# Slot attention: W2 and the carried part of o in fp32 on halves of the array's rows, the update of s2 in fp32 on the whole array

## What is computed

```python
s = clip(hs @ Ws1.T @ Ws2.T + bs2, -32, 32)      # heads x rows x 64 slots
es, enz = exp(s), exp(-cumlogsumexp(s))
A  = mask(q @ k.T * scale)
ok = enz * (A @ es)                              # rows x slots
qv = softmax(ok)
W2 = mask((qv * enz) @ es.T)                     # rows x rows, contraction over 64 slots
o  = W2 @ v
out = (rmsnorm(o) * g_norm * silu(g)) @ Wo.T
```

## Time and profile before

| | |
|---|---|
| median of three runs | 1559.19 us |
| lowest, highest | 1558.36, 1561.25 us |
| span of the profiled execution | 1558.6 us |
| PE busy | 1510.6 us, 97% |
| PE weight load busy | 1280.0 us, 82% |
| DVE, ACT, POOL busy | 1038.4, 625.5, 648.5 us |
| mean granted clock of TensorE | 0.992 |
| matmul instructions | 8720 |

### The profile page before, as it was taken

How to read it: one execution, slowest core, us unless ns; L and a number is a source line. 1 busy time by engine, 2 the same in 40 slices (tenths; PEclk the granted TensorE clock), 3 DMA queues, 4 the chain that set the end, 5 groups by cost and what they waited for, 6 DMA issues and landing times.

```text
span 1558.6 us, 24100 instructions
## 1 busy us (share of the span) xinstructions
PE 1510.6 (97%) x8720; PEld 1280.0 (82%) x8720; DVE 1038.4 (67%) x1840; ACT 625.5 (40%) x1235; POOL 648.5 (42%) x641
## 2 busy tenths in 40 slices
PE   7899999999899999999899999999999999999988
PEld 3788888888788888888788888888888888888866
DVE  4766657567676766667866666666776675667667
ACT  5433334335333333333433433333533333433346
POOL 2444343444443443444433434334444443444345
PEclk9999999999999999999999999999999999999999
DMA  8420212013221101202311120212222011201123
GB/s 321 173 78 23 71 44 71 22 62 114 71 71 45 63 29 39 75 27 86 133 49 45 37 77 22 71 44 92 83 68 75 29 64 44 71 22 45 62 81 122
DMA packets 51444, 109.88 MB, mean 70 GB/s; under 512 B 5376, under 2 KB 15616, under 8 KB 46976
## 3 DMA queue, kind: packets, MB, share of 16 engines
q1 hardware_dynamic: 49088, 104.94, 20.1%
q10 hardware_dynamic: 2304, 4.20, 0.7%
HBM read 86.84 MB, written 26.21 MB: 73 GB/s over the span
## 4 chain that ended last, share of the span: by engine, by line
PE 70%; issue 9%; DVE 8%; ACT 6%; POOL 5%; DMA 1%; POOLq 0%; SPq 0%; DVEq 0%; ACTq 0%
PE bank_qv L859 21%; PE bank_kg L859 20%; PE bank_t L873 5%; PE bank_s L977 3%; PE bank_a L859 3%; PE bank_a L896 3%; PE bank_o L1046 3%; PE bank_s L979 3%; PE bank_c L1058 2%; PE bank_o L859 2%; PE bank_s L859 2%; DVE pT_lo L628 2%; ACT pT_hi L475 2%; ACT batch_raw L475 2%; DVE pair_pT_lo L628 1%
## 5 line engine op out<-in xcount | busy, mean ns | idle before, releaser
L395 POOL TENSOR_TENSOR hs_lo<-hs_raw,hs_hi 128x512 fp32r<-128x512 f32 x64 | 81.5, 1274 | 362.5 <-ACT hs_hi L475 362.5
L859 PE MATMUL bank_qv<-w_hi,hs_hi 128*128 128x512 f32 x512 | 210.2, 411 | 12.8 <-issue 6.6
L859 PE MATMUL bank_kg<-w_hi,hs_hi 128*128 128x512 f32 x512 | 208.2, 407 | 1.0 <-DVE rope_b L648 1.0
L859 PE MATMUL bank_qv<-w_hi,hs_lo 128*128 128x512 f32 x512 | 204.4, 399 | 0.0
L859 PE MATMUL bank_qv<-w_lo,hs_hi 128*128 128x512 f32 x512 | 204.2, 399 | 0.0
L859 PE MATMUL bank_kg<-w_hi,hs_lo 128*128 128x512 f32 x512 | 202.2, 395 | 0.0
L859 PE MATMUL bank_kg<-w_lo,hs_hi 128*128 128x512 f32 x512 | 202.2, 395 | 0.0
L475 ACT ACTIVATE oT_hi<-bank_t 128x512 fp32r<-128x512 f32 x65 | 38.8, 597 | 331.6 <-PE bank_t L873 331.6
L400 POOL TENSOR_TENSOR q_rot<-rope_a,rope_b 128x512 f32<-128x512 f32 x64 | 82.3, 1286 | 187.7 <-DVE rope_b L648 187.7
L628 DVE TENSOR_TENSOR pT_lo<-bank_t,pT_hi 64x256 fp32r<-64x256 f32 x128 | 54.0, 422 | 123.3 <-ACT pair_pT_hi L475 122.2
L390 POOL TENSOR_TENSOR v_lo<-batch_raw,ws_low 128x512 fp32r<-128x512 f32 x64 | 82.6, 1290 | 115.0 <-ACT ws_low L475 114.8
(11 more groups left out here) (190 smaller groups left out, 3757.3 us busy)
## 6 DMA issues: line engine op xcount, KB each, us to landing
w_raw<-w_groups SPq DMA_DIRECT2D x32, 1024.0 KB, 4.9
x_scratch<-part SPq DMA_DIRECT2D x65, 256.0 KB, 2.0
hs_raw<-hs_cols SPq DMA_DIRECT2D x64, 256.0 KB, 2.7
part<-x_scratch SPq DMA_DIRECT2D x64, 256.0 KB, 3.1
batch_raw<-hs_cols SPq DMA_DIRECT2D x4, 1024.0 KB, 7.7
u_part<-u_scratch SPq DMA_DIRECT2D x64, 64.0 KB, 2.4
w_raw<-x_scratch SPq DMA_DIRECT2D x16, 256.0 KB, 2.7
x_scratch<-hs_rows SPq DMA_DIRECT2D x1, 3840.0 KB, 16.0
```

What stands on the lines that cost most here:

```text
L395: pool.tensor_tensor(hs_lo[slot][:, :], hs_raw[slot][:, :], hs_hi[slot][:, :].bitcast(F32), ALU.subtract).then_inc(hs_lo_made, 1)
L859: mm = pe.matmul(dst, x, y, start=start and n == 0, stop=stop and n == 2, **kw)
```

## The change

- **W2** becomes four F32 calls (eight matmul instructions), one for each head, with contraction over 64 rows. Head h uses rows 0 to 63 (h even) or 64 to 127 (h odd) of the array and of `esT` and `pT`, which are now plain 128 x 256 F32 tiles, without zeros and without splits.
- **The carried part of o** becomes four such calls on the same halves, with `pT` stationary and `s2` moving. It moves from behind `masked` times v to right behind W2, ahead of `w2_mm`, for which DVE's mask waits.
- **s2** becomes two F32 calls (four instructions), es by v, 256 columns wide, on all 128 rows.
- **PSUM.** `bank_s` and `bank_o` become one tensor, `bank_wo`, of two banks: even heads in the first, odd ones in the second, W2 in columns 0 to 255 of each bank, o in 256 to 511. `slots_acc`, the place of `ok` and of the slots, is in the part of the first bank that o uses later. The out-projection writes `bank_a`, where W2 was.
- **Waits.** W2 waits for `pT_made` (one ACT copy) and for the clip of the next step's slots. `masked` times v waits for the mask alone; the wait for `part_made` stands ahead of the scores. The k transposes wait for ACT's `esT` copy, no longer for a subtraction of DVE.
- **Gone:** on ACT two half copies and a whole one (in place of three, one), and the copy of v; on DVE two subtractions for `pT_lo`, one for `pair_pT_lo`, one for `esT_lo`, two for `s2_lo`; on POOL `v_lo`, and four memsets at the start.

```diff
-                pe.wait_ge(pT_lo_made, i)
-                for r in range(HG // 2):
-                    mm = product(bank_a[:, 2 * P * r:2 * P * r + 2 * P], cols((esT_hi, esT_lo), P * r, P),
-                                 cols((pT_hi, pT_lo), 2 * P * r, 2 * P))
+
+                pe.wait_ge(pT_made, i)
+                if left:
+                    pe.wait_ge(s_clipped, n)
+                for h in range(HG):
+                    rows, at = slice(64 * (h % 2), 64 * (h % 2) + 64), slice(P * (h // 2), P * (h // 2) + P)
+                    mm = pe.matmul(w2_of(h), esT[rows, at], pT[rows, at], start=True, stop=True)
+                if c:
+                    pe.wait_ge(s2_made, carried(u, c - 1))
+                    for h in range(HG):
+                        rows, at = slice(64 * (h % 2), 64 * (h % 2) + 64), slice(P * (h // 2), P * (h // 2) + P)
+                        mm = pe.matmul(o_of(h), pT[rows, at], s2[rows, at], start=False, stop=False,
+                                       skip_group_check=True)
                 mm.then_inc(w2_mm, 1)
...
                 pe.wait_ge(w2_masked, i)
-                pe.wait_ge(part_made, i)
                 for h in range(HG):
                     head = slice(P * h, P * h + P)
-                    mm = pe.matmul(bank_o[:, head], masked[:, head], v[now][:, head], start=h == 0, stop=c == 0,
+                    mm = pe.matmul(o_of(h), masked[:, head], v[now][:, head], start=False, stop=True,
                                    skip_group_check=True)
-                if c:
-                    pe.wait_ge(s2_lo_made, carried(u, c - 1))
-                    for r in range(HG // 2):
-                        mm = product(bank_o[:, 2 * DV * r:2 * DV * r + 2 * DV],
-                                     cols((pair_pT_hi, pair_pT_lo), P * r, P), cols((s2_hi, s2_lo), 2 * DV * r, 2 * DV),
-                                     start=False, skip_group_check=True)
                 mm.then_inc(o_mm, 1)
...
-                    pe.wait_ge(v_lo_made, i)
                     for r in range(HG // 2):
-                        mm = product(bank_s2[:, 2 * DV * r:2 * DV * r + 2 * DV],
-                                     cols((es_hi[now], es_lo[now]), P * r, P),
-                                     cols((v_hi[now], v_lo[now]), 2 * DV * r, 2 * DV),
-                                     start=c == 0 and r == 0, skip_group_check=True)
+                        pair = slice(2 * DV * r, 2 * DV * r + 2 * DV)
+                        mm = pe.matmul(bank_s2[:, pair], es[now][:, P * r:P * r + P], v[now][:, pair],
+                                       start=c == 0 and r == 0, stop=True, skip_group_check=True)
                     mm.then_inc(s2_mm, 1)
                 if left:
+                    pe.wait_ge(part_made, i)
                     scores(n)
```

More of the change, by code:

```diff
@@ L99, in gated_slot_attention_block @@
         k_rot = [sb(f"k_rot{s}", F) for s in range(2)]
-        v_lo = [sb(f"v_lo{s}", F, F32R) for s in range(2)]
         es_hi = [sb(f"es_hi{s}", H, F32R) for s in range(2)]
         es_lo = [sb(f"es_lo{s}", H, F32R) for s in range(2)]
-        esT_hi, esT_lo = sb("esT_hi", H, F32R), sb("esT_lo", H, F32R)
+        esT = sb("esT", H)
         enz = sb("enz", H)
@@ L106, in gated_slot_attention_block @@
         eps_sum, var, rms = sb("eps_sum", HG), sb("var", HG), sb("rms", HG)
-        pT_hi, pT_lo = sb("pT_hi", F, F32R), sb("pT_lo", F, F32R)
-        pair_pT_hi, pair_pT_lo = sb("pair_pT_hi", H, F32R), sb("pair_pT_lo", H, F32R)
-        s2_hi, s2_lo = sb("s2_hi", HG * DV, F32R), sb("s2_lo", HG * DV, F32R)
+        pT, s2 = sb("pT", H), sb("s2", H)
         o_gated = sb("o_gated", F)
@@ L380, in _ @@
                 pool.memset(t[:, :], 1.0).then_inc(ones_set, 1)
[L381 removed]
+            for t in (wo_hi, wo_lo):
                 pool.memset(t[:, :].bitcast(F32), 0.0).then_inc(zeroed, 1)
@@ L583, in step @@
                     from_bank(v[(c + 1) % 2][:, :], bank_qv[:, :], v_mm, n, v_made)
[L584 to L589, removed]
+                from_bank(pT[:, :], bank_t[:, 0:H], pT_mm, i, pT_made)
                 if last and c == 2:
@@ L796, in step @@
                     w_split(WG, g * 4 + 8)
-                dve.wait_ge(pT_hi_made, i)
-                minus_pair(pT_lo, pT_hi, P, lambda half: per_head(bank_t[64 * half:64 * half + 64, 0:H], 2))
-                minus_hi(pair_pT_lo[:, :], bank_t[:, 0:H], pair_pT_hi[:, :]).then_inc(pT_lo_made, 1)
                 if not left:
@@ L827, in step @@
                 if left:
-                    mask(a_mm, n, a_masked)
-                if c < CB - 1:
-                    dve.wait_ge(s2_hi_made, carried(u, c))
-                    minus_pair(s2_lo, s2_hi, DV, lambda half: of_pair(bank_s2[:, :], half, DV)
-                               ).then_inc(s2_lo_made, 1)
+                    mask_a(n)
                 if c == 0:
@@ L930, in _ @@
             pe.wait_ge(u_made, BATCH)
-            pe.matmul(bank_s[:, 0:H], u_part[0][:, :], ws2_part[:, 0:H], start=True, stop=True).then_inc(s_mm, 1)
+            pe.matmul(slots_acc, u_part[0][:, :], ws2_part[:, 0:H], start=True, stop=True).then_inc(s_mm, 1)
             w_ready(4)
@@ L998, in step @@
                     pe.wait_ge(u_in[nxt], (u * 2 + ((c + 1) // 2 + 1)) * 16)
-                    pe.matmul(bank_s[:, 0:H], u_part[nxt][:, :], ws2_cols(g, last and c == CB - 1), start=True,
+                    pe.matmul(slots_acc, u_part[nxt][:, :], ws2_cols(g, last and c == CB - 1), start=True,
                               stop=True).then_inc(s_mm, 1)
```

106 lines of the change are left out of this document (53 added, 53 removed).

## The result

| | before | after |
|---|---|---|
| median beside each other on one chip | 1558.78 us | 1540.93 us |
| lowest, highest | 1556.67, 1561.25 | 1538.48, 1542.13 |
| ratio, 95% interval | | 0.9884 [0.9869, 0.9898] |
| span of the profiled execution | 1558.6 | 1538.2 |
| PE busy | 1510.6 | 1493.0 |

The changed kernel is 1.2% faster, 17.9 us by the medians and 20.4 us by the two spans. The forecast was 1536 us. Executions of one kernel differ by several microseconds, and the long ones have the lower mean granted clock of TensorE: seven of the kernel before, beside each other on another chip, took from 1555.2 us (at 0.995) to 1562.1 us (at 0.992).

The account below looks back on a forecast made before the run. PE's chain of blocks was taken as the bound: 139.6 us go and 119.3 come, -20, with the ends -23, so 1559.2 - 23 = 1536 us. The range was 1513 to 1580 us.

Parts of the forecast that it names:

- Ends: Program start and last step: the wait for esT_lo goes and the last chain shortens, counted as 3 us together.
- What goes, and the bound: A change is worth what it takes off PE plus the 0.26 us wait ahead of W2; 139.6 us go.
- Side by side: W2 and carried part: row halves work at once, 1.01 us for both; with switch around 0.16, chance 0.36.
- in turn: W2 and carried part: each instruction takes 0.112 us, 0.90 us per block; chance 0.11 with free switch, 0.17 with switches.
- Four calls take 5 paces, because PE takes them in order.: W2 or carried part: eight instructions take 5 paces, 0.56 us; both blocks together 9 paces, 1.01 us.
- The switch, 0.32 us a step: Going to row halves ahead of W2 and back ahead of the es transposes: 0.16 us each, 20.5 us in all.
- the dear case: Each switch costs 0.27 us, since its weight load isn't hidden either; 14 us more, 1550 us; chance 0.12.
- over 0.34: With halves working at once, a switch would have to cost over 0.34 us for the kernel to be slower.
- Forecast +0.09: s2 as four F32 instructions of 0.215 us: 0.86 us where 0.77 stood, 41.3 us against 37.0 over 48 steps.
- The next thing to be late is kT at c = 3 ... at most 0.1 us in 16 steps.: Scores at c = 3 might wait for ACT's kT copy, at most 1.6 us in all; nothing was counted.
- Loop forecast -20: Whole loop: 119.3 us of new PE work and switches against 139.6 us that go.
- Signs in the profile: Expected after: W2 starts in close couples, no engine waited for ahead of W2, DVE busy about 58%.

Follow-up runs that it names:

- the kernel without halves: Kernel after with W2 and the carried part as F32 calls on all 128 rows, two of 256 columns each, block-diagonal operands: 1565.81 us, ratio 1.0049.
- one half only: Kernel after with all heads of W2 and of the carried part on rows 0 to 63: 1587.24 us, ratio 1.0181.
- the early split: ACT's input split moved ahead of its wait for project g, behind the esT copy: kernel before 1551.52 us, kernel after 1526.72 us.

## Why the prediction was right, point by point

Direction, range and size held: 1536 forecast, 1541 measured. The forecast was -23 us; the spans differ by 20.4, of which 2.6 are no part of the change (see "Ends"), and the medians by 17.9. But the steps below it don't all hold. That it came out so close is in part luck: a miss of 9 us and one of 6 had opposite signs.

- **What goes, and the bound.** Right. PE's turn is what counts, the 0.26 us wait ahead of W2 went in all 64 steps, and DVE's 146 us of work less were worth that wait (17 us) and no more in the loop: the kernel without halves has the same relief and is 0.5% slower than before, with PE busy for 97% of it as well.
- **Side by side or in turn.** Right, and the choice that mattered: 46 us lie between them (one half only). The argument for "in turn", a weight load that does not shorten, was right about one half: 0.112 us on 64 rows too. The row that the prediction read for it (0.84 us) had 64 moving columns and full 128-row loads, so it said nothing of rows; the run on one half does. That the halves would share one load path was wrong.
- **"Four calls take 5 paces, because PE takes them in order."** Wrong. It takes 4 (W2) and 8 (both), not 5 and 9; with heads 2 and 1 swapped in the order W2 still takes 4. The step that failed is "in order"; its size, one pace of 0.11 us a visit, is small beside the choice above.
- **The switch, 0.32 us a step.** Right in size: 0.09 as a longer gap ahead of W2 (0.318 against 0.228), 0.10 for a first load that nothing hides, 0.10 behind the last couple and 0.06 in the es transposes, 0.35 together, and 0.40 when a second visit was added. Its make-up was another: the prediction gave 0.16 to each side, for the record's tail, and left the unhidden load (0.10) to the dear case; in fact that load is paid, and only part of the tail. The Trainium skill (TensorEngine Tiling, Key Properties) says that a change of mode drains the array. The run fits that, with this price, but not as a wait for the record's end: the es transposes start 0.203 us after the last couple, whose records last 0.272 (the ends of these records are modelled). Side by side and with a switch of 0.34 us the prediction's own sum comes to no change; slower by 0.2% it is from 0.37 on, so its "over 0.34" is a little low.
- W2, carried part, wait and switch together: forecast -0.45 us for c > 0 and -0.19 for c = 0, measured -0.54 and -0.28 (table above). 64 x 0.09 = 6 us better than forecast.
- **s2.** Forecast +0.09, measured +0.12, and +0.03 in s1 ahead of it. 48 x 0.06 = 3 us worse. The pace of 0.215 was right and is the 0.86 of the kernel without halves for the same shape; what was missed stands at its start: the second instruction comes 0.272 us after the first, the others at 0.216, and the first comes 0.112 us after s1's last where the F32R one came after 0.085. Why is open.
- **"The next thing to be late is kT at c = 3 ... at most 0.1 us in 16 steps."** The size was right: masked times v takes 0.993 us there, 0.10 more, 1.5 us in all. But the sentence named the wrong *next*. The wait for `hs_lo` was in the view of the waits of before already, 12 times, and the move of the carried part shortened just its cover. Cost: 0.62 x 15 = 9 us. The prediction followed ACT's and DVE's work that the moved block touches, and not the transfers and splits for the next sequence that happened to lie beside its old place.
- **Ends, -3.** Too small, by about 2 us. The first scores come 1.4 us sooner, since the wait for `esT_lo` ahead of them is gone. The first step is 2.7 us shorter in the traces (24.3 to 21.6), but that is not the change. In the profiled execution of before the granted clock stood at 0.5 (1.2 GHz) from 46.0 to 52.9 us, after PE had stood still for 1.4, 1.0 and 2.2 us in short order, and the scores and project q fell into it; from the chain that ended last:

```profile
47.27 2.07 PE bank_a L896 x8
49.34 4.45 PE bank_qv L859 x12
```

  At 2.4 GHz these two blocks hold 1.16 and 2.80 us, in after and in the trace of the kernel before with the early split alike, and there the first step of the old code takes 21.7 us: 2.6 us came from the clock of one execution. From the last scores to the end it is 3.5 us less. In that stretch too before's trace has 3.4 us at 1.2 GHz (1503.5 to 1506.9), after PE had stood still for 1.3 and 1.4:

```profile
1503.07 4.62 PE bank_o L859 x12
```

  At full clock such a block holds 2.75, so 1.9 of the 3.5 us are the clock. All three traces with the old W2 have such a stretch behind the last scores, and one of the nine others, so it may come with the change; that isn't shown. The remaining 1.6 are about what the prediction named there (0.43 and 0.72).
- **The sum again.** Loop forecast -20; pairs and switch -6; s2 +3; `hs_lo` +9; `kT` +1.5: -12.5. The trace shows -12.8 in the loop. With -1.4 and -3.5 at the ends that makes -17.7, where the medians differ by 17.9; the rest of the -20.4 of the spans is the clock in before's first step.
- **Signs in the profile.** DVE at 58%: right. Close couples: right, but four full ones, not the first of one head with the second of the one before. "PE waits for nobody ahead of W2": right. The gap behind the last `Wo` was to be 0.23 if the switch was free, and is 0.318; the one ahead of the es transposes was to be 0.11, and is 0.203. No sign of being wrong was set on `hs_lo`, where the miss was.

What stays open: how far ahead of program order a free half may run (one swapped order was tried), whether halves pair in one PSUM bank too (no run has two halves of the rows in one), and why s1's last instruction and s2's first hold PE longer beside an F32 s2.

## What to carry to other kernels

When the contraction is over 64, put neighbouring calls on alternate halves of the rows (here in different PSUM banks), and put everything that works on halves in one place of the loop: a pair costs one pace, a visit to halves costs three to four. When you move a block out of a stretch, list every wait that ends in that stretch on whatever engine works toward it, above all at the steps that lack other blocks (here c = 3, without s1 and s2); here a wait of 0.3 us that already showed in the view of the waits took 0.62 us of the 0.71 of cover that went. A split on engines with time to spare is no reason to take a dearer product on the busy one (s2: 5 us). And before two profiled executions are subtracted from each other, compare their granted clock stretch by stretch: here it made 2.6 us of a difference of 20.4.

## What the runs showed of the hardware

- Two F32 matmuls on different 64-row halves start 7 ns apart, their weight loads with them, and the couples follow at 0.105 to 0.112 us. On one half alone the pace is 0.112 for each instruction.
- With 64 stationary columns a call, halves of the columns pair in the same way: eight instructions in 0.587 us instead of four wider ones in 0.919.
- A visit to row halves and back costs 0.35 to 0.40 us at full clock, in four places: a longer gap (0.09), an unhidden first load (0.10), and 0.10 and 0.06 behind the last couple.
- Instructions for the free half start ahead of program order: with four of one half in front, the eight of W2 still start within 0.45 us, in each of 64 steps, where strict order needs 0.67.
- An F32 call costs two instructions of 0.112 us with 128 moving columns and of 0.216 with 256; an F32R matmul with 256 moving columns costs 0.12. So three F32R ones (0.36) are cheaper than one F32 call (0.43) at 256 columns.
